# Four edits in the order of a decoder's big attention on one core: who splits the experts' weights, when a bias is added, who makes a chunk's low part, and where one sum P·V stands

## The chip, the cores and the metric

The kernel runs on one core of one Trainium2 chip. The metric is the device time of one execution in microseconds (us). Engines are named as in the profile: PE is TensorE's matmuls, PEld its weight loads, DVE VectorE, ACT ScalarE, POOL GpSimd (Pool), SP the engine that issues the DMAs.

## The reference

A decoder layer on x (16 sequences x 128 positions x 256), float32 throughout:

```python
x = _layernorm(x + attn(x, Wqkv, bqkv, Wo, bo))                   # A: 16 heads of 16
x = _layernorm(x + xattn(x, mask, ctx, Wq, Wk, Wv, Wo, gate))     # B: 32 heads of 8, gated adapter
x = _layernorm(x + ffn(x, ...))
# ffn: h = x + attention(layernorm(x)*w1 + b1)    16 heads of 128, rotary, causal softmax, biases
#      h + moe(layernorm(h)*w2 + b2)              4 experts 256 -> 256 -> 256, top 2, exact gelu
```

The change lies in the ffn's attention (the "big attention", stage C) and its passage to the experts (stage D).

## The kernel before

**Precision.** Where both sides of a product need float32 accuracy, each is kept as a high part (a copy rounded to fp32r by ScalarE) and a low part (value minus high part), and three products are summed: high x high, high x low, low x high. So the weights need a "split": `split_high` (L1709, ScalarE) and `split_low` (L1622, a subtraction of 128 x 1024 elements, by VectorE or Pool). The same is done for the normalized input of a chunk: `xt_pe` transposes it (L1454), `xt_act` scales it (L1472), `xh_act` makes the high part (L1479) and `xt_pool` the low part (L1486, two instructions of 128 x 512, t = 0 and 1).

**Stage C.** 64 units u = 0..63. A unit is one head (r = u % 16) on one chunk of four sequences (c = u // 16), 512 positions wide. The projections of head v run two units ahead, in unit v - 2. All engines walk the same loop over u, each through its own queue, in the order written, with semaphores between them:

- TensorE (`pe_c`): scores of u (L1526); transposition of the probabilities of u-1 (`turn`, L1540); query projection of u+2 (`project_c` with kq 0, L1497 to L1499, six products 128 x 512); output projection of u-2 (`out_proj`, L1566 to L1568); P·V of u-1 (`pv`, L1553); key projection of u+2 (kq 1); values of u+2 (L1513 to L1515). In a chunk's unit r = 14 the query projection belongs to the next chunk, whose input must first be there: it stands behind P·V. In r = 12 the next chunk's input is transposed.
- VectorE (`dve_c`): causal mask and row maxima of u (L1648, `maxima_c`); rotation with bias of the query projection (`rope_c` with kq 0, L1635 twice and L1638); after a chunk's end the residual (L1673); reciprocal of the sums (L1666); low part of the attention's output of u-1 (`out_low`, L1659); rotation of the key projection (kq 1); splits of the experts' weights in units 55 to 58; one step of the next chunk's layer norm for r = 4..11 (L1430 to L1443).
- ScalarE (`act_c`): copy of the transposed probabilities (L1718), exponentials (L1727), high part of the output (`out_high`, L1735), copy of the values (L1746), `split_high` in units 0 to 11 and 55 to 58, and for r = 12, 13 the next chunk's input and its high part.
- Pool (`pool_c`): the rotation's sum into the query buffer (`rope_sum_c`, L1794, kq 0), scaling of the probabilities (`soft`, L1802), the rotation's sum for the key; then `split_low` in units 0 to 11; `add_bias` (L1810, 128 x 256, one sequence); the power for the norm (L1449, r = 7); the low part of the next chunk's input (r = 13).

**What waits for what.** A projection or values product takes one of two PSUM banks in turn (`turn_bank`), and waits until the one before last in that order is read: the values of u+2 for the query's rotation, the query projection of u+3 for the key's rotation. `turn` waits for `soft`. P·V waits for ScalarE's copy, the high output for P·V, VectorE's low output for the high output. The first products of a chunk wait for both halves of the low part (`xt_ready`). The weights of the experts (DW) come in four halves (k = 16..19) through two staging buffers, the next load issued when a half is split. After the last chunk, unit 62 runs the first expert product (`hidden_pe`, L1930) in place of the values, which waits for the low part of chunk 4.

Of the kernel before, what the change touches and what calls it, by code (L numbers as in the profile page):

```python
# [6 lines left out]
F32 = mybir.dt.float32  # L7
F32R = mybir.dt.float32r
BF16 = mybir.dt.bfloat16
ALU = mybir.AluOpType  # L10
# [33 lines left out]
def program(nc, I, out):  # L44
    ctx = ExitStack()
    sem = Sems(nc, ctx)
# [998 lines left out]
    def pool_ab(e, steps):  # L1045
        q = Queue(e, sem)

        def init_values(b, n):

            if (b, n) in ((0, 0), (0, 1)):  # L1050
                q.wait_ge("w_dve", 4)
            elif (b, n) == (3, 1):
                q.wait_ge("z_dve", 16)
                q.wait_ge("rp_cos", 16)
            else:
                k = {(1, 0): 8, (1, 1): 6, (2, 0): 0, (2, 1): 2, (3, 0): 4}[b, n]
                for k in (k, k + 1):
                    q.wait_ge("pv_pe", last_unit(k + 10 if k < 6 else k, 0) + 1)
            k = 6 * (2 * b + n)
            vp = VPB[n][b].rearrange("p (t h) x -> p t h x", t=2)  # L1060
            e.memset(VPB[n][b], 0.0).then_inc(sem("z_B"), 1)
            q.wait_ge("z_B", k + 1)
            for i in range(3):
                e.memset(vp[:, :, i:12:3, 24 + i:25 + i], 1.0).then_inc(sem("z_B"), 1)
            e.memset(vp[:, 0, 12:16, 24:27:2], 1.0).then_inc(sem("z_B"), 1)
            e.memset(vp[:, 1, 12:16, 25:27], 1.0).then_inc(sem("z_B"), 1)

        def add_adapter(g):
            q.wait_ge("on_dve", on_v(out_group(g, 1), 4))
            e.tensor_tensor(ON[:, :], ON[:, :], OS, ALU.add).then_inc(sem("n_pool"), 1)  # L1070

        def mask_low(c):
            q.wait_ge("mkh_act", c - 7)
            if c >= 10:
                q.wait_ge("s_pe", last_unit(2 * (c - 2) + 1, 0) + 1)
            e.tensor_tensor(MKl[c % 2][:, :, :], MK[c % 2], MKh[c % 2][:, :, :].bitcast(F32), ALU.subtract).then_inc(sem("mkl_pool"), 1)

        def add_bias(g):
            q.wait_ge("ld_m", 48)
            q.wait_ge(f"ld_x{g // 2}", 16)  # L1080
            q.wait_ge("xt_pe", g // 2 + 1)
            e.tensor_tensor(X[:, g, :], X[:, g, :], boA, ALU.add).then_inc(sem("xb_pool"), 1)

        def weights_low(n):
            q.wait_ge("w_act", n + 1)
            e.tensor_tensor(Wl[0][:, :, piece(0, n)], staged(0, n), Wh[0][:, :, piece(0, n)].bitcast(F32),
                            ALU.subtract).then_inc(sem("w_pool"), 1)

        if steps.start < 0:
            for i in range(10):  # L1090
                e.memset(VPA[i], 0.0).then_inc(sem("z_A"), 1)
            q.wait_ge("z_A", 10)
            e.memset(VPOOL[:, 0:160, 16:17], 1.0).then_inc(sem("z_A"), 1)
        for s in steps:
            if s == 3 - AHEAD:
                weights_low(2)
            if s == 4 - AHEAD:
                weights_low(3)
            if s in INITS:
                init_values(*INITS[s])  # L1100
            if s - 1 in ends and ends[s - 1][0] < 16:
                add_bias(ends[s - 1][0])
            if s - 2 in tos and tos[s - 2][1]:
                add_adapter(tos[s - 2][0])
            if s - 2 in masked:
                mask_low(masked[s - 2][0])
            for part in range(2):
                if s in splits[part] and splits[part][s] not in FIRST:
                    split(e, q, *splits[part][s], part)
            if s in ropes and ropes[s][1] < 2 and ropes[s] not in FIRST:  # L1110
                rope(e, q, *ropes[s])
                if ropes[s][0] >= 9:
                    rope_cos(e, q, *ropes[s])
            if s in sums and sums[s][1] < 2 and sums[s] not in FIRST:
                rope_sum(e, q, *sums[s])
            if s in shifts and shifts[s] >= 16:
                shift_parts(e, q, shifts[s], "sh_pool")
            if s - 2 in wos:
                g = wos[s - 2]
                layernorm_power(e, q, g, "ln")  # L1120
                if g >= 16:
                    layernorm_apply(e, q, X[:, g - 16, :], z[:, :], g, "ln").then_inc(sem("x_done"), 1)
            if s == NORMS[3] + 1:
                norm_pool(e, q, 0)
            if s in NORMS[4:]:
                norm_step(e, q, 0, NORMS.index(s))
            if s in LOWS[:2]:
                split_low(e, q, LOWS.index(s))
            if s == X_LOW:
                for t in range(2):  # L1130
                    xt_pool(e, q, 0, t)
            for (v, kq), step in ROPES.items():
                if s == step:
                    rope_sum_c(e, q, v, kq)
# [161 lines left out]
    XF = [sb("C_XF", [128, 2, 512], F32, st_d)]  # L1296
    XCh = [sb("C_XTh", [128, 2, 512], F32R, st_d)]
# [60 lines left out]
    NU, NCH = 64, 4  # L1358
# [51 lines left out]
        return bank[4 + key[1]] if key[0] == "v" else home["cp", key[1], key[2]]  # L1410

    def xt_ready(c):
        return "xl_pool", 2 * c + 2

    def prep(u):

# [61 lines left out]
        q.wait_ge("xf_act", 2 * c + t + 1)  # L1478
        e.activation(XCh[i][:, t, :], XF[i][:, t, :], ACT.Copy).then_inc(sem("xh_act"), 1)  # L1479

    def xt_pool(e, q, c, t):
        i = 0 if c < 5 else c % 2
        if c == 0:
            q.wait_ge(*LEFT[1])
        q.wait_ge("xh_act", 2 * c + t + 1)
        e.tensor_tensor(XCl[i][:, t, :], XF[i][:, t, :], XCh[i][:, t, :].bitcast(F32), ALU.subtract).then_inc(sem("xl_pool"), 1)  # L1486

    def project_c(e, q, v, kq, o=None):
        c, r = divmod(v, 16)
# [39 lines left out]
    def pe_c(e):  # L1529
# [41 lines left out]
        for u in range(NU):  # L1571
            if u >= 2:
                scores_c(e, q, u)
            if u == NU - 1:
                gate_pe(e, q, 0)
            if u:
                turn(u - 1)
            if u == 0:
                q.wait_ge("z_dve", 32)
                q.wait_ge("rc_dve", 4)  # L1580
            if u + 2 < NU and u % 16 != 14:
                project_c(e, q, u + 2, 0)
            if u == NU - 1:
                hidden_pe(e, q, 0, 1)
            if u >= 2:
                out_proj(u - 2)
            if u:
                pv(u - 1)
            if u + 2 < NU and u % 16 == 14:
                project_c(e, q, u + 2, 0)  # L1590
            if u + 2 < NU:
                project_c(e, q, u + 2, 1)
                values_c(e, q, u + 2)
            else:
                hidden_pe(e, q, 0, 0 if u == NU - 2 else 2)
            if u % 16 == 12:

                q.wait_ge("oc_dve", u)
                for t in range(2):
                    xt_pe(e, q, u // 16 + 1, t, bank[2 + t])  # L1600
# [12 lines left out]
    def split_low(e, q, k):  # L1613
        hi, lo, src = half(k)
        if k in (2, 3):
            q.wait_ge(*LEFT[3])
        if k in (2, 4, 16):
            q.wait_ge("cw_low", k)
        if k in (16, 17):
            q.wait_ge("yc_pe", 54)  # L1620
        q.wait_ge("cw_act", k + 1)
        e.tensor_tensor(lo, src, hi.bitcast(F32), ALU.subtract).then_inc(sem("cw_low"), 1)  # L1622
# [29 lines left out]
    def dve_c(e):  # L1652
# [23 lines left out]
        for u in range(NU + 2):  # L1676
            c, r = divmod(u, 16)
            if 2 <= u < NU:
                maxima_c(e, q, u)
            if u == NU - 1:  # L1680
                gate_dve(e, q, 0, 0)
            if u + 2 < NU:
# [9 lines left out]
                    norm_step(e, q, 5, 4 * (u - NU + 2) + k)  # L1692
            if u + 2 < NU:
                rope_c(e, q, u + 2, 1)
            if c == 3 and 7 <= r <= 10:
                split_low(e, q, 16 + r - 7)
            if c < 4 and 4 <= r < 12:
                norm_step(e, q, c + 1, r - 4)
            if u == NU:
# [96 lines left out]
    def pool_c(e):  # L1796
# [15 lines left out]
        for u in range(NU):  # L1812
            c, r = divmod(u, 16)
            if u + 2 < NU:
                rope_sum_c(e, q, u + 2, 0)
            soft(u)
            if u + 2 < NU:
                rope_sum_c(e, q, u + 2, 1)
            if u < 12:
                split_low(e, q, 4 + u)  # L1820
            if 0 <= r - (8 if c else 12) < 4:
                add_bias(4 * c + r - (8 if c else 12))
            if r == 7:
                norm_pool(e, q, c + 1)
            if r == 13:
                for t in range(2):
                    xt_pool(e, q, c + 1, t)
            if u == NU - 2:
                norm_pool(e, q, 5)
        hidden_pool(e, q, 0, 0)  # L1830
        for m in range(1, 5):
            hidden_pool(e, q, 0, m)
        xt_pool(e, q, 5, 0)
        hidden_pool(e, q, 0, 5)
        xt_pool(e, q, 5, 1)
        hidden_pool(e, q, 0, 6)
        hidden_pool(e, q, 0, 7)

# [30 lines left out]
    XT_FIRST = 5  # L1869
# [288 lines left out]
    def pool_d(e):  # L2158
# [12 lines left out]
        for c in range(1, NCH):  # L2171
            for m in range(8):
                if c + 1 < NCH and XT_FIRST <= m < XT_FIRST + 2:
                    xt_pool(e, q, c + 5, m - XT_FIRST)
                hidden_pool(e, q, c, m)
                if c + 1 < NCH and m == 1:
                    norm_pool(e, q, c + 5)
# [187 lines left out]
```

## Time and profile before

| | us |
|---|---|
| three runs | 1230.07, 1232.98, 1234.13 |
| median | 1232.98 |
| the profiled execution | 1232.17 |
| its span (first to last instruction) | 1230.4 |
| mean granted TensorE clock | 0.985 |
| PE busy | 1146.7 (93%) |
| DVE busy | 986.4 (80%) |
| ACT busy | 656.9 (53%) |
| POOL busy | 660.3 (54%) |

Stage C runs from about 580 to 1100 us of the span. In the rows of the trace a line stands for all the buffers of a name; an entry in square brackets is the idle time of the engine before the instruction, and what ended it. An instruction's time on record can include a wait that the engine makes within it. "Unit u" begins in the text with its first scores product (L1526): unit 8 at 644.39, unit 13 at 684.68, unit 14 at 692.53, unit 15 at 704.66, unit 30 at 824.16, unit 31 at 834.79, unit 56 at 1036.44, unit 61 at 1083.40, unit 62 at 1091.25.

### The profile page before, as it was taken

The numbers are of one execution on the slowest core, as the hardware profiler recorded it, in microseconds if no ns is written. First come the engines' busy times: TensorE is split into PE (matmuls) and PEld (weight loads), VectorE is DVE, ScalarE is ACT, GpSimd is POOL, SyncE is SP. The second block draws the span as 40 slices with busy tenths as digits, with TensorE's granted clock in tenths as the row PEclk, the third lists the DMA queues.
The fourth block names the chain that finished last, engine by engine and source line by source line (L and its number), as shares of the span: only waits on it lengthen the run. The fifth ranks groups of instructions, "written<-read, shape, count | busy, mean of one in ns | idle before, by whom it ended". The sixth has DMA issues, their size and how long they took to land.

```text
span 1230.4 us, 29543 instructions
## 1 busy us (share of the span) xinstructions
PE 1146.7 (93%) x11172; PEld 938.6 (76%) x11172; DVE 986.4 (80%) x2274; ACT 656.9 (53%) x1687; POOL 660.3 (54%) x714
## 2 busy tenths in 40 slices
PE   5799999899999999878999999999999999899998
PEld 5676666566666666555899899988999898788886
DVE  6767786888888888967888688878888788966877
ACT  5365554566667667464555444453444444457663
POOL 4566556435455455253778544554455444556665
PEclk9899999999999999989999999999999999998999
DMA  8754543343333333302121000000000100001111
GB/s 228 184 133 116 125 122 84 84 103 103 94 103 102 95 101 88 106 18 78 61 69 53 1 1 2 1 2 1 1 2 1 35 2 18 19 3 35 35 35 35
DMA packets 98558, 76.22 MB, mean 62 GB/s; under 512 B 73547, under 2 KB 86987, under 8 KB 98417
## 3 DMA queue, kind: packets, MB, share of 16 engines
q1 hardware_dynamic: 98417, 74.34, 22.6%
q8 instruction: 89, 1.46, 0.5%
q14 instruction: 52, 0.43, 0.1%
HBM read 53.40 MB, written 19.92 MB: 60 GB/s over the span
## 4 chain that ended last, share of the span: by engine, by line
PE 61%; DVE 22%; issue 7%; ACT 4%; POOL 4%; DMA 1%; SPq 0%; DVEq 0%; POOLq 0%; ACTq 0%
PE bank L1497 4%; PE bank L1498 4%; PE bank L1499 4%; PE bank L607 4%; PE bank L1553 4%; PE bank L1526 4%; DVE B_nr L732 3%; DVE PT L741 3%; PE bank L543 3%; PE bank L550 2%; PE bank L470 2%; PE bank L1513 2%; PE bank L585 2%; PE bank L1515 2%; PE bank L1514 2%
## 5 line engine op out<-in xcount | busy, mean ns | idle before, releaser
L1794 POOL TENSOR_TENSOR C_QK<-C_t1b,C_t2b 128x512 f32<-128x512 f32 x128 | 167.0, 1305 | 240.6 <-DVE C_t2b L1638 240.4
L1635 DVE SCALAR_TENSOR_TENSOR C_t1b<-bank,C_bcol,C_tabs 64x512 f32<-64x512 f32 x256 | 192.0, 750 | 52.1 <-PE bank L1499 47.9
L732 DVE TENSOR_REDUCE B_nr<-bank 128x4 f32<-128x512 f32 x256 | 164.4, 684 | 34.4 <-PE bank L550 33.3
L1497 PE MATMUL bank<-C_XTh,C_Wh 128*128 128x512 f32 x256 | 113.7, 444 | 6.8 <-POOL C_XTl L1486 4.5
L972 ACT ACTIVATE PT<-bank 128x512 f32<-128x512 f32 x160 | 92.0, 597 | 50.7 <-PE bank L585 50.5
L1746 ACT ACTIVATE C_V<-bank 128x512 f32<-128x512 f32 x64 | 38.1, 598 | 149.2 <-PE bank L1515 147.6
L965 ACT ACTIVATE PT<-PT 128x512 f32<-128x512 f32 x96 | 59.5, 631 | 93.9 <-DVE PT L741 93.9
L1727 ACT ACTIVATE C_P<-bank,C_nm 128x128 f32<-128x128 f32 x256 | 90.7, 367 | 35.0 <-DVE C_nm L1648 33.3
L1498 PE MATMUL bank<-C_XTl,C_Wh 128*128 128x512 f32 x256 | 102.4, 400 | 0.0
L1499 PE MATMUL bank<-C_XTh,C_Wl 128*128 128x512 f32 x256 | 102.2, 399 | 0.0
L607 PE MATMUL bank<-PT,vpool 128*32 128x128 f32 x2048 | 97.3, 285 | 3.9 <-ACT PT L965 3.7
L1638 DVE SCALAR_TENSOR_TENSOR C_t2b<-bank,C_bcol,C_tabs 128x512 f32<-128x512 f32 x128 | 96.1, 751 | 1.8
L550 PEld LDWEIGHTS bank<-stk 48*128 48x128 bf16 (+1 forms) x1280 | 49.5, 95 | 47.3 <-issue 25.7
L585 PE MATMUL bank<-stk 54*128 54x128 bf16 (+1 forms) x1280 | 76.1, 218 | 7.2 <-DVE PT L741 5.0
L550 PE MATMUL bank<-stk 48*128 48x128 bf16 (+1 forms) x1280 | 76.2, 219 | 5.9 <-DVE B_nr L732 5.8
L1513 PE MATMUL bank<-C_Wh,C_XTh 128*128 128x256 f32 x256 | 72.9, 285 | 8.1 <-DVE C_t2b L1638 8.0
L1735 ACT ACTIVATE C_OTh<-bank,C_bcol 128x512 fp32r<-128x512 f32 x64 | 44.2, 690 | 66.6 <-PE bank L1553 65.8
L1659 DVE SCALAR_TENSOR_TENSOR C_OTl<-bank,C_bcol,C_OTh 128x512 fp32r<-128x512 f32 x64 | 47.7, 745 | 37.0 <-ACT C_OTh L1735 37.0
L438 POOL TENSOR_TENSOR PB<-y,PB 128x512 bf16<-128x512 f32 x37 | 43.3, 1170 | 56.0 <-ACT PB L916 55.7
L585 PEld LDWEIGHTS bank<-stk 54*128 54x128 bf16 (+1 forms) x1280 | 53.1, 95 | 25.4 <-DVE PT L741 8.2
L1514 PE MATMUL bank<-C_Wl,C_XTh 128*128 128x256 f32 x256 | 71.9, 281 | 0.0
L1566 PE MATMUL bank<-C_Wh,C_OTh 128*128 128x256 f32 x256 | 71.9, 281 | 0.0
(267 smaller groups left out, 3678.0 us busy)
## 6 DMA issues: line engine op xcount, KB each, us to landing
Adrq<-PB SPq DMA_DIRECT2D x16, 192.0 KB, 2.8
Adrk<-PB SPq DMA_DIRECT2D x16, 192.0 KB, 2.9
stk<-Adrq SPq DMA_DIRECT2D x16, 192.0 KB
stk<-Adrk SPq DMA_DIRECT2D x16, 192.0 KB
Bdrq<-PB SPq DMA_DIRECT2D x16, 192.0 KB, 2.9
stk<-Bdrq SPq DMA_DIRECT2D x32, 96.0 KB
Bdrk<-PB SPq DMA_DIRECT2D x16, 192.0 KB, 2.6
stk<-Bdrk SPq DMA_DIRECT2D x32, 96.0 KB
```

The source lines that it names most:

```text
L550: m = e.matmul(bank[n % 2][:, j * 128:j * 128 + 128], QS[L][i3][rows, h, :], (AS if kd else KS[L])[i3][rows, h, :], start=bool(kd), stop=b ...
L585: m = e.matmul(bank2(n)[:, j * 128:j * 128 + 128], (AS if kd else KS[L])[i3][rows, h, :], QS[L][i3][rows, h, :], start=bool(L), stop=bool( ...
L607: m = e.matmul(o[32 * j:32 * j + 32, c3 * 128:c3 * 128 + 128], vp[:, h, :], pt_of(n)[:, j * 128:j * 128 + 128], start=first or not L, stop ...
L732: e.tensor_reduce(dst, bank[n % 2][:, :].rearrange("p (a b) -> p a b", a=4), AX.X, ALU.max, negate=True).then_inc(sem("m_dve"), 1)
L1497: e.matmul(o[:, :], CWh[hp][:, cs], XCh[0][:, t, :], start=t == 0, stop=False)
L1498: e.matmul(o[:, :], CWh[hp][:, cs], XCl[0][:, t, :], start=False, stop=False)
L1499: m = e.matmul(o[:, :], CWl[hp][:, cs], XCh[0][:, t, :], start=False, stop=t == 1)
L1513: e.matmul(ob, XCh[0][:, t, xs], CWh[hp][:, cs], start=t == 0, stop=False)
L1514: e.matmul(ob, XCh[0][:, t, xs], CWl[hp][:, cs], start=False, stop=False)
L1635: e.scalar_tensor_tensor(out=v4(t1b[kq][lo:lo + 64, :]), in0=v4(o[hi:hi + 64, :]), scalar=bc[hi:hi + 64, :], in1=tabsC[hi:hi + 64, 2 * kq ...
L1638: e.scalar_tensor_tensor(out=v4(t2b[kq][:, :]), in0=v4(o[:, :]), scalar=bc, in1=tabsC[:, 2 * kq, :].unsqueeze(1).to_broadcast([128, 4, 128 ...
L1794: e.tensor_tensor(QK[v % 3][:, kq, :], t1b[kq][:, :], t2b[kq][:, :], ALU.add).then_inc(sem("rc_pool"), 1)
```

## The change

`xt_pool` becomes `xt_low` (semaphore `xl_done`) and can be issued by either engine. The rest, cut to its core:

```diff
 # pe_c
-            if u:
+            if u and (u % 16 != 14 or u + 2 >= NU):
                 pv(u - 1)
             if u + 2 < NU and u % 16 == 14:
                 project_c(e, q, u + 2, 0)
             if u + 2 < NU:
                 project_c(e, q, u + 2, 1)
+                if u % 16 == 14:
+                    pv(u - 1)
                 values_c(e, q, u + 2)
 # split_low
-        if k in (2, 4, 16):
+        if k in (2, 4):
             q.wait_ge("cw_low", k)
 # dve_c
                 maxima_c(e, q, u)
+            if r == 14:
+                xt_low(e, q, c + 1, 1)
             ...
                 rope_c(e, q, u + 2, 1)
-            if c == 3 and 7 <= r <= 10:
-                split_low(e, q, 16 + r - 7)
 # pool_c
                 split_low(e, q, 4 + u)
-            if 0 <= r - (8 if c else 12) < 4:
-                add_bias(4 * c + r - (8 if c else 12))
+            if c == 3 and 7 <= r <= 10:
+                split_low(e, q, 16 + r - 7)
             if r == 7:
                 norm_pool(e, q, c + 1)
             if r == 13:
-                for t in range(2):
-                    xt_pool(e, q, c + 1, t)
+                xt_low(e, q, c + 1, 0)
+            if 0 <= r - (0 if c else 12) < 4:
+                add_bias(4 * c + r - (0 if c else 12))
```

So: the four low parts of the experts' weights are made by Pool; the output bias is added to the residual rows in r = 0..3 of chunks 1 to 3 (in chunk 0 still in r = 12..15, but behind the low part); of the next chunk's low part Pool makes t = 0 in r = 13 and VectorE t = 1 in r = 14, behind its maxima; and in r = 14 of chunks 0 to 2 P·V stands behind both projections, in front of the values.

## Rows read from the trace of the kernel before

**Rows 1.** The page, part 4: the chain that ended last, by engine.
```profile
PE 61%; DVE 22%; issue 7%; ACT 4%; POOL 4%; DMA 1%; SPq 0%; DVEq 0%; POOLq 0%; ACTq 0%
```
**Rows 2.** Stretches (length, busy us (instructions) of each engine, PEclk, DMA).
```profile
644.39:684.68 40.29, 40.29 (x290) 37.48 (x289) 35.19 (x89) 21.83 (x62) 31.13 (x21) 1.00 0.15 42
1036.44:1083.40 46.96, 42.34 (x290) 37.25 (x289) 43.54 (x93) 20.55 (x61) 24.80 (x20) 1.00 0.08 24
684.68:692.53 7.85, 7.85 (x59) 7.30 (x57) 5.59 (x16) 4.07 (x12) 4.27 (x4) 1.00 0.00 0
692.53:704.66 12.13, 9.93 (x59) 8.44 (x57) 5.96 (x17) 4.22 (x13) 5.92 (x6) 0.86 0.01 1
...
824.16:834.79 10.63, 8.40 (x59) 7.31 (x58) 5.97 (x17) 4.22 (x13) 5.25 (x5) 1.00 0.01 2
...
954.29:964.91 10.62, 8.39 (x58) 7.31 (x57) 5.97 (x17) 4.22 (x13) 5.25 (x5) 1.00 0.33 101
```
**Rows 3.** Waits of PE in stage C: total, times, longest.
```profile
PE bank L1513 <- DVE C_t2b L1638: 8.0, 8, 1.2
```
**Rows 4.** Line L1622, the low part of weights: ns min/median/max, first and last start.
```profile
L1622 POOL TENSOR_TENSOR C_Wl<-C_z,C_Wh x6: 2375/2390/2397, 592.1 to 670.7; 128x1024 fp32r<-128x1024 f32 x6
```
**Rows 5.** Timeline of Pool and VectorE, unit 56 (start, duration, instruction).
```profile
1047.23 1.29 POOL L1794 TENSOR_TENSOR C_QK<-C_t1b,C_t2b 128x512 f32<-128x512 f32 x1 [0.74 <-DVE C_t2b L1638]
1048.48 1.73 POOL L1810 TENSOR_TENSOR X<-X,C_bo 128x256 f32<-128x256 f32 x1
...
1047.47 2.13 DVE L1622 TENSOR_TENSOR C_Wl<-C_XF,C_Wh 128x1024 fp32r<-128x1024 f32 x1 [0.32 <-ACT C_Wh L1709]
```
**Rows 6.** VectorE's subtractions of two widths, before stage C, by line and form.
```profile
L714 DVE TENSOR_TENSOR B_Wl<-vpool,B_Wh 128x1024 fp32r<-128x1024 f32 x2 | 2.4, 1220 | 1.9 <-ACT B_Wh L862 1.9
...
L714 DVE TENSOR_TENSOR A_Wl<-stk,A_Wh 128x512 fp32r<-128x512 f32 x2 | 1.3, 682 | 0.0
```
**Rows 7.** Timelines of unit 30: TensorE, VectorE, ScalarE, Pool.
```profile
826.91 1.05 PE L1553 MATMUL bank<-C_PT,C_V 128*128 128x128 f32 x8
829.22 0.50 PE L1497 MATMUL bank<-C_XTh,C_Wh 128*128 128x512 f32 x1 [1.26 <-POOL C_XTl L1486]
...
833.27 0.39 PE L1513 MATMUL bank<-C_Wh,C_XTh 128*128 128x256 f32 x1 [0.97 <-DVE C_t2b L1638]
...
826.22 0.14 DVE L1648 DVE_READ_ACCUMULATOR2_ANT C_nm<- 128x1 f32 x1
...
833.21 0.72 DVE L1659 SCALAR_TENSOR_TENSOR C_OTl<-bank,C_bcol,C_OTh 128x512 fp32r<-128x512 f32 x1
833.97 0.76 DVE L1635 SCALAR_TENSOR_TENSOR C_t1b<-bank,C_bcol,C_tabs 64x512 f32<-64x512 f32 x1
...
828.00 0.69 ACT L1735 ACTIVATE C_OTh<-bank,C_bcol 128x512 fp32r<-128x512 f32 x1
...
825.42 1.30 POOL L1794 TENSOR_TENSOR C_QK<-C_t1b,C_t2b 128x512 f32<-128x512 f32 x1 [1.50 <-DVE C_t2b L1638]
826.67 2.50 POOL L1486 TENSOR_TENSOR C_XTl<-C_XF,C_XTh 128x512 fp32r<-128x512 f32 x2
```
**Rows 8.** The same of unit 14: Pool, VectorE, TensorE.
```profile
693.78 1.30 POOL L1794 TENSOR_TENSOR C_QK<-C_t1b,C_t2b 128x512 f32<-128x512 f32 x1 [1.50 <-DVE C_t2b L1638]
695.04 0.72 POOL L1810 TENSOR_TENSOR X<-X,C_bo 128x256 f32<-128x256 f32 x1
...
703.84 0.76 DVE L1635 SCALAR_TENSOR_TENSOR C_t1b<-bank,C_bcol,C_tabs 64x512 f32<-64x512 f32 x1
...
698.26 0.50 PE L1497 MATMUL bank<-C_XTh,C_Wh 128*128 128x512 f32 x1 [1.93 <-POOL C_XTl L1486]
...
703.14 0.39 PE L1513 MATMUL bank<-C_Wh,C_XTh 128*128 128x256 f32 x1 [0.27 <-DVE C_t2b L1638]
```
**Rows 9.** The same of unit 62: Pool, TensorE.
```profile
1092.50 1.29 POOL L1794 TENSOR_TENSOR C_QK<-C_t1b,C_t2b 128x512 f32<-128x512 f32 x1 [1.50 <-DVE C_t2b L1638]
...
1096.30 0.50 PE L1930 MATMUL bank<-C_XTh,C_Wh 128*128 128x512 f32 x1 [1.26 <-POOL C_XTl L1486]
```

More of the change, by code:

```diff
@@ L1130, in pool_ab @@
                 for t in range(2):
-                    xt_pool(e, q, 0, t)
+                    xt_low(e, q, 0, t)
             for (v, kq), step in ROPES.items():
@@ L1412, in xt_ready @@
     def xt_ready(c):
-        return "xl_pool", 2 * c + 2
+        return "xl_done", 2 * c + 2
     def prep(u):
@@ L1479, in xh_act, with xt_low @@
         e.activation(XCh[i][:, t, :], XF[i][:, t, :], ACT.Copy).then_inc(sem("xh_act"), 1)
-    def xt_pool(e, q, c, t):
+    def xt_low(e, q, c, t):
         i = 0 if c < 5 else c % 2
@@ L1485, in xt_pool @@
         q.wait_ge("xh_act", 2 * c + t + 1)
-        e.tensor_tensor(XCl[i][:, t, :], XF[i][:, t, :], XCh[i][:, t, :].bitcast(F32), ALU.subtract).then_inc(sem("xl_pool"), 1)
+        e.tensor_tensor(XCl[i][:, t, :], XF[i][:, t, :], XCh[i][:, t, :].bitcast(F32), ALU.subtract).then_inc(sem("xl_done"), 1)
     def project_c(e, q, v, kq, o=None):
@@ L1832, in pool_c @@
             hidden_pool(e, q, 0, m)
-        xt_pool(e, q, 5, 0)
+        xt_low(e, q, 5, 0)
         hidden_pool(e, q, 0, 5)
-        xt_pool(e, q, 5, 1)
+        xt_low(e, q, 5, 1)
         hidden_pool(e, q, 0, 6)
@@ L2173, in pool_d @@
                 if c + 1 < NCH and XT_FIRST <= m < XT_FIRST + 2:
-                    xt_pool(e, q, c + 5, m - XT_FIRST)
+                    xt_low(e, q, c + 5, m - XT_FIRST)
                 hidden_pool(e, q, c, m)
```

## The prediction

> **What bounds the kernel now.** I read the page's busy shares and chain first, then the stretches of the big attention, then TensorE's waits there, then single units. The chain of work that ended last is 61% TensorE and 22% VectorE [rows 1]. A regular unit of the big attention takes 7.85 us, with 7.85 us of TensorE in it [rows 2]: so there only what makes TensorE stand still counts. It stands still in two places that the change touches. It waits 8.0 us in all at the value products (L1513) for VectorE's rotation [rows 3], and 1.93 us [rows 8] and 1.26 us [rows 7] at the first projection of a chunk (L1497) for Pool's low part. The stretches [rows 2] say when. Units 56 to 60 take 46.96 us, while units 8 to 12, with the same 290 products, take 40.29. And the last-but-one unit of a chunk takes 12.13, 10.63 and 10.62 us instead of 7.85.
>
> **The experts' weights (four splits from VectorE to Pool in units 55 to 58).** The same rows price it, because before the change the units 7 to 11 already have the new arrangement: Pool runs one split of 2.39 us in each [rows 4], right behind the second rotation sum, ScalarE makes the high part in front of it, and VectorE does the normalization steps of the next chunk beside. Stretch against stretch: 46.96 - 40.29 = 6.67 us saved [rows 2]. TensorE's value product no longer waits, because VectorE's order (maxima, rotation, low output, rotation) is no longer shifted by the split (2.13 us for the second one [rows 5]). What hides Pool's 2.39 us is Pool's own idle time: 31.13 us busy of 40.29 with the splits in place. The heaviest moment is the first split, with the power of the norm now queued behind it; its twin is inside the stretch too, since what Pool does last in unit 7 runs after the scores of unit 8 have begun. The twin stretch has five splits, the new one will have four. No wait is new in front of the split: it stands behind a rotation sum that needs a later projection than the out product it waits for. The load of the next half of the weights is issued after the split as in the first chunk. Bounds of this term: 7.7 (46.96 less five regular units of 7.85) and -8.1 (four splits of 2.39 and the rotation sums of 1.30 behind them, all exposed).
>
> **Bias in a chunk's first units.** Four additions of 0.72 us on Pool move from r = 8..11 to r = 0..3 in chunks 1 to 3. Pool idles 1.5 us or more before its rotation sums in both places, and what reads the biased rows (the residual) comes in the next chunk. 0, between -0.1 and +0.3. In chunk 0 the addition of r = 13 goes behind the low part, which is in the next step.
>
> **Low part in halves, one on VectorE.** Chunk 1 to 2 first [rows 7]. Pool's rotation sum ends at 826.72, then come both halves, 2.50 us, and the first projection starts at 829.22. VectorE has finished its maxima at 826.36 and is then idle until that projection, so the half costs VectorE nothing. If the halves ran side by side, the low part would be done at 826.72 + 1.25 = 827.97. But both instructions read two operands from SBUF, and the trace shows what happens then [rows 5]: VectorE's split starts at 1047.47 under a Pool addition that ends at 1048.52, and ends at 1049.60, 1.08 us after it, though it is on record as 2.13 us; Pool's bias, queued at 1048.48, ends at 1050.21, 0.61 us after VectorE let go, though it takes 0.72 alone. They exclude each other. So: VectorE's half is queued at 826.38 behind the running Pool sum. It runs after 826.72 for 1.08 us less the difference between 1024 and 512 columns (1.22 - 0.68 = 0.54 [rows 6]), to 827.26. Pool's half follows, 1.25 - 0.11 = 1.14 us, to 828.40; the projection starts 0.05 later, at 828.45: 0.77 us earlier, not 1.20.
>
> The Trainium skill (SBUF — State Buffer, section Who interferes with whom) has this as an exclusive lock between a VectorE instruction with two SBUF inputs and a GpSimd one that reads SBUF, given to whoever issues first. The trace agrees on the exclusion by the 1.08 us. If Pool's half got it first, the end would be 827.97 + 0.54 = 828.51, 0.11 later; without any exclusion it would be 827.97.
>
> **The sum P·V placed later.** In unit 30 TensorE now does both projections (3.08 us, 829.22 to 832.30 before, so 828.45 to 831.53), then P·V (1.05 us, overlapping 0.16: to 832.42). Behind P·V hang ScalarE's high output (starts 0.04 later, 0.69 us: 833.15) and VectorE's low output (0.72 us, from 833.18 to 833.90), and in VectorE's queue the second rotation stands behind that low output: it starts at 833.94. Before it started at 833.97. TensorE's next projection needs the bank that this rotation reads. So of the 0.77 us nothing is left: 0.03 us a boundary, for chunks 1 to 2 and 2 to 3. TensorE's 0.97 us wait before the value products goes, and a wait of about 1 us in front of the next unit's projection takes its place. With P·V in its old place the second rotation would keep its distance of 4.75 us from the first projection (829.22 to 833.97) and start at 833.20.
>
> Chunk 0 to 1 [rows 8]: Pool's sum ends at 695.08, and the bias (0.72 us) is out of the way. VectorE's half to 695.62, Pool's to 696.76, projection at 696.81 instead of 698.26. The idle time of TensorE becomes 1.4 us instead of 1.93, and I take it that the clock stays up: the granted share was 0.86 in this unit and 1.00 in unit 30, where it had idled 1.26 and 0.97 [rows 2, 7]. Then: projections to 699.89, P·V to 700.78, high output to 701.51, low output to 702.26, second rotation at 702.30 instead of 703.84: 1.54 us saved.
>
> End of chunk 3 [rows 9]: P·V stays in its place there. Pool's sum ends at 1093.79, VectorE's half at 1094.33, Pool's at 1095.47, first hidden product at 1095.52 instead of 1096.30: 0.78 us. What follows (last scores, gate, transposition, exponentials) is a chain through TensorE and ScalarE, so it is kept.
>
> **The sum.** 6.67 + 1.54 + 2 x 0.03 + 0.78 = 9.05 us. The profiled execution took 1232.17 us (span 1230.40), so it becomes 1223.1. The median of the three runs shown is 0.8 above it (1232.98); I go half way: 1223.5.
>
> **Rivals.** (a) The halves do run side by side: 0.43 us more at each of four places, 9.05 + 1.7 = 10.8 us, 1221.8. For it: VectorE is free at the right moment; against it: rows 5. (b) The clock falls at the boundaries. TensorE idles 1.4 us before the projection (out product's end 827.07 to 828.45) and about 1 us again five us later. Twelve projection products took 4.61 us in chunk 0 (698.26 to 702.87) and 3.08 at full clock, so 1.5 us for each of three boundaries: 1225.0 for one, 1228.1 for all. Against it: 1.26 followed by 0.97 us did not bring it down [rows 2, 7]. (c) Pool is too full in units 55 to 58: its soft-max scaling, which releases the transposition, stands behind the split. Its work there is 31.13 / 5 = 6.2 us of a unit's 8.1; a split that waits over some 1.9 us for its high part, or for the lock, pushes the scaling out and stops TensorE. Exposed in part, 1.5 us a unit, it gives 1229.5, which can't be told from no change. (d) The slower case, the same place at full price: Pool's split (2.39) and the rotation sum queued behind it (1.30) are both exposed in all four units, 3.69 x 4 = 14.8 us; 14.8 - 9.05 = +5.7, 1238.3. It outweighs the rest once a unit grows by over 9.05 / 4 = 2.3 us, so once Pool's wait passes 1.9 + 2.3 = 4.2 us. Against (c) and (d): units 8 to 12 of the first chunk [rows 2].
>
> **Numbers.** Forecast 0.58, (a) 0.13, (b) 0.18, (c) 0.06, (d) 0.02, and 0.03 for something between forecast and no change. The range: 1220.3 (side by side, less the spread of the runs) to 1228.1 (the clock at all boundaries). 0.3%, about what a measurement of this kernel tells from no change, is 3.7 us. Faster by more: 0.92 (forecast, a, b and the rest), same 0.06, slower 0.02.
>
> **What would show it.** After the change units 56 to 60 should take 40.3 us, and TensorE's wait at L1513 for the rotation should be near zero. VectorE's half should be on record with about 0.9 us (0.34 of it a wait) and Pool's with some 1.7. In unit 30 the value products should begin about 0.8 us earlier, and so the long unit be 9.9 us instead of 10.63, but the first projection of unit 31 not: that unit should be as much longer. Units 14 and 15 together should lose 1.5 us. I am wrong on the lock if both halves show their plain 0.68 and 1.25 us, on P·V if the second rotation after a boundary is 0.5 us earlier or more, on the clock if the granted share in the long units of chunks 1 and 2 is under 1.00, and on Pool if TensorE waits at the transposition (L1540) for the scaling.

## The result

| | before | changed |
|---|---|---|
| four runs each, median (range) | 1232.20 (1230.07 to 1234.13) | 1220.74 (1218.70 to 1223.33) |
| ratio, 95% interval | | 0.9909 [0.9883, 0.9934] |
| profiled execution | 1232.17 | 1221.01 |
| its span | 1230.4 | 1219.2 |
| timed again, 11 and 6 runs | 1231.40 | 1224.29 |
| ratio, 95% interval | | 0.9940 [0.9926, 0.9953] |

The change is faster by 11.5 us in one comparison and 7.1 us in the other, 0.9% and 0.6% of the time; 9.05 was the sum and 1223.5 the forecast. The profiles say where the time went. These are stretches of the changed kernel, cut at the first scores product of a unit as in [rows 2] (length, busy us (instructions) of PE, PEld, DVE, ACT and POOL, PEclk, DMA share, GB/s): the first chunk's units 8 to 12, units 56 to 60, then 14, 15, 30, 31, unit 62, all that is before stage C, and all that follows the last scores.

```profile
643.43:683.73 40.30, 40.30 (x290) 37.48 (x289) 35.21 (x89) 21.79 (x62) 31.12 (x21) 1.00 0.14 41
1033.94:1074.05 40.11, 40.11 (x291) 37.38 (x289) 35.20 (x89) 20.97 (x61) 28.76 (x20) 1.00 0.10 28
...
691.58:701.41 9.83, 8.38 (x58) 7.45 (x57) 6.24 (x17) 4.22 (x13) 5.16 (x5) 1.00 0.01 2
701.41:710.30 8.89, 8.12 (x59) 7.35 (x58) 7.38 (x18) 3.39 (x11) 5.08 (x5) 1.00 0.00 1
821.70:831.53 9.83, 8.38 (x59) 7.44 (x58) 6.24 (x17) 4.22 (x13) 4.47 (x4) 1.00 0.01 3
831.53:840.41 8.88, 8.11 (x58) 7.34 (x57) 7.37 (x18) 3.39 (x11) 4.37 (x4) 1.00 0.00 1
...
1081.89:1087.66 5.77, 5.29 (x40) 4.85 (x39) 4.44 (x15) 4.22 (x13) 3.97 (x3) 1.00 0.00 0
0.00:579.02 579.02, 520.57 (x6896) 372.20 (x6897) 459.80 (x937) 344.64 (x839) 298.06 (x402) 0.98 0.41 108
1087.66:1219.20 131.54, 123.32 (x763) 105.10 (x761) 99.22 (x261) 77.90 (x123) 79.05 (x82) 0.97 0.10 33
```

The same view of the kernel before, where it was not shown: before stage C, units 15 and 31, and the end.

```profile
0.00:579.96 579.96, 520.45 (x6897) 372.39 (x6898) 460.77 (x937) 344.06 (x839) 297.02 (x402) 0.98 0.41 108
704.66:712.80 8.14, 8.14 (x59) 7.35 (x58) 6.64 (x17) 3.39 (x11) 5.08 (x5) 1.00 0.00 1
834.79:842.92 8.13, 8.11 (x59) 7.34 (x58) 6.63 (x17) 3.40 (x11) 4.37 (x4) 1.00 0.00 1
...
1097.80:1230.38 132.58, 124.67 (x763) 106.25 (x761) 97.25 (x258) 77.96 (x123) 79.11 (x82) 0.96 0.10 33
```

| stretch | before | changed | difference | forecast |
|---|---|---|---|---|
| units 56 to 60 | 46.96 | 40.11 | -6.85 | -6.67 |
| 14 + 15 (chunk 0 to 1) | 20.27 | 18.72 | -1.55 | -1.54 |
| 30 + 31 (chunk 1 to 2) | 18.76 | 18.71 | -0.05 | -0.03 |
| 46 + 47 (chunk 2 to 3) | 18.74 | 18.73 | -0.01 | -0.03 |
| unit 62 | 6.55 | 5.77 | -0.78 | -0.78 |
| before stage C | 579.96 | 579.02 | -0.94 | 0 |
| after the last scores | 132.58 | 131.54 | -1.04 | 0 |

Stage C gave 9.24 us. Only part of the 6.85 us of units 56 to 60 is idle time of TensorE: it stood still for 4.62 us in this stretch before ([rows 2], length less PE busy); the other 2.23 us are in the recorded time of the same products, 42.34 us before and 40.11 after. A sum of waits would have missed them, the comparison of stretches did not.

The other 2 us of this profile lie where the change does nothing. The work there is the same, but for three short instructions of VectorE that were done before the last scores and now come behind them; TensorE's instructions keep their distance from the last scores to 0.01 us for the next 14 us, so the 0.78 us of unit 62 is kept. What differs in the last stretch is the granted clock, 0.96 against 0.97, with PE busy 124.67 against 123.32 us. In the ten other profiles the part before stage C took 577.6 to 581.3 us and the part after the last scores 130.8 to 133.0. That is no effect of the change: the changed kernel itself, in the profile of the second comparison, took 581.16 and 132.85 us there, and its stage C is the same to 0.1 us in every stretch of the table. So 9.2 us is what the change does in stage C, and 7 to 11 is what single comparisons of whole runs show of it. The interval of the second comparison (5.8 to 9.1 us) ends just short of 9.2; why whole runs gave less there than in the first comparison isn't settled beyond these two stretches.

Unit 30 of the changed kernel, to set beside [rows 7] (start, duration, instruction; in brackets the idle time before it). All of it lies 2.47 us earlier, by what was saved up to there.

```profile
825.97 0.50 PE L1497 MATMUL bank<-C_XTh,C_Wh 128*128 128x512 f32 x1 [1.37 <-POOL C_XTl L1486]
...
828.87 1.05 PE L1553 MATMUL bank<-C_PT,C_V 128*128 128x128 f32 x8
830.01 0.39 PE L1513 MATMUL bank<-C_Wh,C_XTh 128*128 128x256 f32 x1
...
833.79 0.50 PE L1497 MATMUL bank<-C_XTh,C_Wh 128*128 128x512 f32 x1 [0.77 <-DVE C_t2b L1640]
```
```profile
823.75 1.04 DVE L1486 TENSOR_TENSOR C_XTl<-C_XF,C_XTh 128x512 fp32r<-128x512 f32 x1
...
830.68 0.75 DVE L1661 SCALAR_TENSOR_TENSOR C_OTl<-bank,C_bcol,C_OTh 128x512 fp32r<-128x512 f32 x1 [0.64 <-ACT C_OTh L1737]
831.46 1.51 DVE L1637 SCALAR_TENSOR_TENSOR C_t1b<-bank,C_bcol,C_tabs 64x512 f32<-64x512 f32 x2
```
```profile
829.96 0.69 ACT L1737 ACTIVATE C_OTh<-bank,C_bcol 128x512 fp32r<-128x512 f32 x1 [4.53 <-PE bank L1553]
```
```profile
822.95 1.30 POOL L1796 TENSOR_TENSOR C_QK<-C_t1b,C_t2b 128x512 f32<-128x512 f32 x1 [1.50 <-DVE C_t2b L1640]
824.20 1.72 POOL L1486 TENSOR_TENSOR C_XTl<-C_XF,C_XTh 128x512 fp32r<-128x512 f32 x1
```

The reader is to see three things. VectorE's half is on record from 823.75 to 824.79, but Pool's rotation sum ran until 824.25: 0.54 us behind it, as worked out. (It had been queued before VectorE's last maxima instruction was through, so it is on record with 1.04 us, not the 0.9 that was forecast.) Pool's half takes 1.72 us instead of 1.25 and ends at 825.92; the first projection starts at 825.97, which is 828.44 in the time of before (forecast 828.45). VectorE's second rotation starts at 831.46, 833.93 in the time of before (forecast 833.94). The wait before the values (0.97) has become one before the next unit's projection (0.77). TensorE's waits in stage C, of which L1513 was 8.0 us [rows 3]:

```profile
PE bank L1497 <- POOL C_XTl L1486: 4.1, 3, 1.4
PE bank L1497 <- DVE C_t2b L1640: 3.1, 6, 0.8
PE bank L1513 <- DVE C_t2b L1640: 1.3, 1, 1.3
```

The wait that is left at L1513 lies at 587.57 us, at the start of stage C, where the kernel before had one of 1.23 us too; the seven others are gone.

### The profile page after: what moved, and what is told of

It is laid out like the page before. It is cut to its first block, busy times and chain, and to the rows that moved or that the text cites. A ratio compares the mean times of both kernels' runs of the same rounds, so it can differ in the third digit from the quotient of the medians.

```text
span 1219.2 us, 29543 instructions
## 1 busy us (share of the span) xinstructions
PE 1141.6 (94%) x11172; PEld 936.7 (77%) x11172; DVE 982.3 (81%) x2274; ACT 657.6 (54%) x1687; POOL 664.7 (55%) x714
## 4 chain that ended last, share of the span: by engine, by line
PE 63%; DVE 21%; issue 7%; ACT 4%; POOL 4%; DMA 1%; SPq 1%; DVEq 0%; POOLq 0%; ACTq 0%
PE bank L1497 5%; PE bank L1498 5%; PE bank L1499 5%; PE bank L1553 4%; PE bank L1526 4%; PE bank L607 4%; DVE B_nr L732 3%; DVE PT L741 3%; PE bank L543 3%; PE bank L550 2%; PE bank L470 2%; PE bank L1568 2%; PE bank L1567 2%; PE bank L1566 2%; PE bank L585 2%
## 5 line engine op out<-in xcount | busy, mean ns | idle before, releaser
L1637 DVE SCALAR_TENSOR_TENSOR C_t1b<-bank,C_bcol,C_tabs 64x512 f32<-64x512 f32 x256 | 192.0, 750 | 45.5 <-PE bank L1499 41.5
L1513 PE MATMUL bank<-C_Wh,C_XTh 128*128 128x256 f32 x256 | 72.5, 283 | 1.6 <-DVE C_t2b L1640 1.3
```

Of the source, the lines that this page charges most:

```text
L1637: e.scalar_tensor_tensor(out=v4(t1b[kq][lo:lo + 64, :]), in0=v4(o[hi:hi + 64, :]), scalar=bc[hi:hi + 64, :], in1=tabsC[hi:hi + 64, 2 * kq ...
```

## The experiments

Each is the changed kernel with the edit shown. The compared quantity is the length of the stretches, since it doesn't move with the clock of the other stages. Where no median is given, the version ran once.

**P·V back in front of the projections.**
```diff
-            if u and (u % 16 != 14 or u + 2 >= NU):
+            if u:
                 pv(u - 1)
 ...
-                if u % 16 == 14:
-                    pv(u - 1)
                 values_c(e, q, u + 2)
```


> The changed kernel with P·V of r = 14 back in front of the projections. My theory (the second rotation hangs on P·V through the high and the low output): the first projection of a chunk starts where it does in the changed kernel, but the second rotation starts 4.75 us after it instead of 5.5, so units 14+15, 30+31 and 46+47 are 0.75 us shorter each (18.0 instead of 18.7 us), 2.2 us in all: about 1218.5. Rival (the late P·V fills TensorE's wait before the values and so is worth it): the same or up to 1 us a boundary longer.

Units 14+15, 30+31 and 46+47 (18.72 us in the changed kernel, forecast 18.0):

```profile
693.92:711.88 17.96, 16.51 (x114) 14.65 (x113) 13.50 (x34) 7.62 (x24) 10.25 (x9) 1.00 0.00 1
823.24:841.21 17.97, 16.52 (x115) 14.66 (x114) 13.51 (x34) 7.62 (x24) 8.85 (x7) 1.00 0.01 2
952.61:970.58 17.97, 16.52 (x114) 14.65 (x113) 13.49 (x34) 7.62 (x24) 8.86 (x7) 1.00 0.19 59
```

The place of P·V costs 0.75 us at each boundary. The median of 4 runs is 1219.94 (forecast 1218.5), ratio to before 0.9905 [0.9889, 0.9922]; the whole times alone don't part it from the changed kernel (0.9909), the stretches do. Unit 30 itself, from 823.24 to 833.09, is as long as with P·V late (9.85 against 9.83 us); it is unit 31 that is shorter, 8.12 against 8.88. TensorE waits longer in front of the values now, 0.97 us at each of the three boundaries (the fourth wait, 1.24 us, is the one at the start of stage C), and is faster all the same, because it waits less at the projections:

```profile
PE bank L1513 <- DVE C_t2b L1638: 4.2, 4, 1.2
PE bank L1497 <- POOL C_XTl L1486: 1.4, 3, 0.5
PE bank L1497 <- DVE C_t2b L1638: 0.8, 3, 0.3
```

**The four splits back on VectorE.**
```diff
 # pool_c
-            if c == 3 and 7 <= r <= 10:
-                split_low(e, q, 16 + r - 7)
 # dve_c, behind the key's rotation
+            if c == 3 and 7 <= r <= 10:
+                split_low(e, q, 16 + r - 7)
 ...
```
(`split_low` waits for `cw_low` at k = 16 again, as before.)

> The changed kernel with the experts' four low parts back on VectorE. My theory: units 56 to 60 take 47.0 us again instead of 40.1, +6.8 us, nothing else moves. Rival (part of the gain there came from the bias being gone from the same units, r = 8 to 11, where it was held up by VectorE's splits): 45.5 us or less.

Units 56 to 60:

```profile
1034.88:1080.55 45.67, 42.35 (x290) 37.25 (x289) 42.27 (x93) 20.54 (x61) 19.04 (x16) 1.00 0.08 24
```

That is neither the 47.0 of my theory nor quite the rival's 45.5. The rival is right in kind: 1.29 us of the 6.85 are gained without moving a split, by the bias alone. The normalization step shows how. Before, and in this run (VectorE, unit 56, one execution each):

```profile
1049.53 0.83 DVE L1443 TENSOR_SCALAR C_XN<-X,mv,rstd 128x256 f32<-128x256 f32 x1
```
```profile
1047.96 0.40 DVE L1443 TENSOR_SCALAR C_XN<-X,mv,rstd 128x256 f32<-128x256 f32 x1
```

Before, Pool's bias waited behind the split [rows 5] and was over at 1050.21, 0.61 us after the split; the step is on record from 1049.53 to 1050.36, and I read its extra 0.43 us as a wait for the bias in turn. The same pair stands in units 56, 57 and 58; in unit 59, where the bias has no split in front of it, the step takes 0.41 us. Three times 0.43 us are 1.29.

**Bias back in r = 8 to 11, splits on Pool.**
```diff
-            if 0 <= r - (0 if c else 12) < 4:
-                add_bias(4 * c + r - (0 if c else 12))
+            if 0 <= r - (8 if c else 12) < 4:
+                add_bias(4 * c + r - (8 if c else 12))
```


> The changed kernel with the bias of chunks 1 to 3 back in r = 8 to 11 (the splits stay on Pool). The run with the splits on VectorE took 45.7 us for units 56 to 60 and not 47.0, with VectorE's normalization step at 0.40 us instead of 0.83: the bias had held the exclusive access that VectorE's split had let go. My theory: with the splits on Pool the step is issued in front of Pool's rotation sum, the bias comes 4 us later and falls into idle time, so units 56 to 60 take 40.1 to 40.3 us and the bias's new place is worth nothing here. Rival (Pool is now so full that 0.72 us more delays its scaling): TensorE waits at the transposition (L1540), 41 us or more.

Units 56 to 60: 40.13 us. Pool is busy 31.39 us in them instead of 28.76, and TensorE without a pause:

```profile
1033.61:1073.74 40.13, 40.13 (x290) 37.40 (x289) 35.19 (x89) 20.96 (x61) 31.39 (x24) 1.00 0.09 28
```

So with the splits on Pool the bias's place is worth nothing in these units, and the splits alone bring the whole 6.8 us. The two edits don't add up: either one removes what the bias did. Nor does the new place cost anything: units 16 to 19, 32 to 35 and 48 to 51 of the changed kernel are as long as before, to 0.02 us each.

**Both halves of the low part on Pool.**
```diff
 # pool_c, r == 13
-                xt_low(e, q, c + 1, 0)
+                for t in range(2):
+                    xt_low(e, q, c + 1, t)
 # dve_c
-            if r == 14:
-                xt_low(e, q, c + 1, 1)
```


> The changed kernel with both halves of the low part on Pool in r = 13 (P·V late). My theory: Pool needs 2.50 us where the two engines need 1.72, so each first projection starts 0.78 us later, and with P·V late all of it is kept: units 30+31 take 19.5 us, which is 0.75 more than even before the change; four places, +3.1 us. If TensorE's idle time of 2.2 us lets its clock fall, 1.5 us more at a boundary. Rival (the second rotation is held by something else than P·V): units 30+31 stay at 18.7.

Units 14+15, 30+31 and 46+47:

```profile
692.50:713.55 21.05, 17.78 (x115) 15.87 (x114) 12.71 (x33) 7.62 (x24) 11.00 (x10) 0.92 0.00 1
824.95:846.01 21.06, 17.80 (x115) 15.98 (x114) 12.71 (x33) 7.62 (x24) 9.61 (x8) 0.92 0.01 2
957.38:976.88 19.50, 16.51 (x114) 14.80 (x113) 12.72 (x33) 7.62 (x24) 9.62 (x8) 1.00 0.17 55
```

The third is the forecast of 19.5 to the digit: 0.77 us over the changed kernel and 0.76 over the kernel before. So the late P·V by itself, with nothing else changed there, makes a boundary slower than it was. In the other two the granted clock fell to 0.92 over the two units, 1.55 us more. All three had the same pause of TensorE in front of the projection, 2.15, 2.14 and 2.14 us:

```profile
962.43 0.50 PE L1497 MATMUL bank<-C_XTh,C_Wh 128*128 128x512 f32 x1 [2.14 <-POOL C_XTl L1486]
```

That is rival (b) of the prediction, in one execution. With the low part in halves the pause is 1.37 us (P·V late) or shorter, and the granted share was 1.00 at every boundary of all eight profiles with halves. The halves are the only edit between this version and the changed kernel, so they are what spared it the longer pause; putting P·V back would have done so too (1.26 us in unit 30 of the kernel before, share 1.00). At the end of chunk 3 unit 62 took 6.55 us here, as before the change, so its 0.78 us are the halves' alone.

**Pool's half in front of the rotation sum, P·V in its old place.**
```diff
 # pool_c (and the P·V edit of the first experiment)
             soft(u)
+            if r == 13:
+                xt_low(e, q, c + 1, 0)
             if u + 2 < NU:
                 rope_sum_c(e, q, u + 2, 1)
-            if r == 13:
-                xt_low(e, q, c + 1, 0)
```


> The changed kernel with P·V in its old place and, in r = 13, Pool's half of the low part in front of the rotation sum of the key instead of behind it (the sum is needed a unit later only). My theory (what delays the low part is the rotation sum in front of it and the exclusion between Pool and VectorE behind it): Pool's half runs while VectorE still makes the maxima, VectorE's half follows, the low part is done before P·V is, and TensorE doesn't wait for it: units 30+31 take 17.3 us instead of 18.7, three times 1.4, and 0.6 at the end of chunk 3: 4.8 us under the changed kernel, about 1216. Rival (the rotation sum, now later, holds up the next scores or the scaling): TensorE waits at the scores (L1526) or the transposition (L1540), and less or nothing is gained.

Units 30+31 (forecast 17.3); 14+15 and 46+47 took 17.23 and 17.22, units 61+62 12.88 (13.62 in the changed kernel):

```profile
818.80:836.02 17.22, 16.24 (x114) 14.58 (x113) 13.64 (x34) 7.62 (x24) 8.87 (x7) 1.00 0.01 2
```

TensorE's wait for the low part is gone; neither the scores nor the transposition waits, but for 0.6 us at the start of stage C that the kernel before has too. Pool and VectorE in unit 30:

```profile
820.19 1.30 POOL L1486 TENSOR_TENSOR C_XTl<-C_XF,C_XTh 128x512 fp32r<-128x512 f32 x1 [1.64 <-ACT C_XTh L1479]
821.45 1.73 POOL L1794 TENSOR_TENSOR C_QK<-C_t1b,C_t2b 128x512 f32<-128x512 f32 x1
```
```profile
820.85 1.19 DVE L1486 TENSOR_TENSOR C_XTl<-C_XF,C_XTh 128x512 fp32r<-128x512 f32 x1
```

VectorE's half ends 0.55 us after Pool's (821.49 to 822.04), once more by the exclusion, and now it is the rotation sum that is held up, for which nobody waits yet. Median 1217.14 (forecast 1216), ratio to before 0.9886 [0.9871, 0.9901]. What the place in front would bring with both halves on Pool was not run.

**The same with P·V late.** (The edit of `pool_c` alone.)

> Pool's half of the low part in front of the key's rotation sum, as in the run before, but with P·V late as in the changed kernel. My theory: the first projection starts 0.26 us sooner than with P·V in front, but the second rotation hangs on P·V (projections, P·V, high output, low output) and starts 0.5 us later: units 30+31 take 17.75 us against 17.22; units 61+62 12.87 as there. Rival (with the low part early the order of P·V makes no difference, or the late one is better since TensorE's 0.98 us wait before the values is filled): 17.2 or less.

Units 30+31, and to 0.01 us the same at the other two boundaries, as forecast; units 61+62 12.87:

```profile
819.47:837.23 17.76, 16.52 (x114) 14.78 (x113) 13.75 (x34) 7.61 (x24) 8.87 (x7) 1.00 0.01 2
```

So the late P·V costs here too, 0.53 us. (Its single run was 1215.28 us, lower than the medians of the version above: its last stretch had the clock at 0.98 and took 130.8 us, where the version above took 133.0.)

**Both halves on VectorE, P·V in its old place.**
```diff
 # dve_c, r == 14
-                xt_low(e, q, c + 1, 1)
+                for t in range(2):
+                    xt_low(e, q, c + 1, t)
 # pool_c: nothing in r == 13
```


> Both halves of the low part on VectorE in r = 14, P·V in its old place. My theory (VectorE waits until Pool's rotation sum is through, then needs 0.54 + 0.68 us, where VectorE and Pool need 0.54 + 1.14): the first projection starts 0.45 us earlier than with one half each, units 30+31 take 17.5 us against 17.96, units 61+62 13.2 against 13.6. Rival (no exclusion, VectorE starts at once): 17.3 or less. Rival (VectorE's extra work delays the maxima or rotation): 18 or more.

Units 30+31 and 46+47: 17.45 us (forecast 17.5), 61+62 13.09 (13.2). Units 14+15 took 17.97, a miss of 0.5: only there Pool has its bias queued behind the rotation sum (r = 13 of chunk 0). VectorE's two halves are on record as one line, and so is the bias:

```profile
693.77 2.18 DVE L1486 TENSOR_TENSOR C_XTl<-C_XF,C_XTh 128x512 fp32r<-128x512 f32 x2
694.22 1.18 POOL L1811 TENSOR_TENSOR X<-X,C_bo 128x256 f32<-128x256 f32 x1
```

The rotation sum ends at 694.27, the bias at 695.40, VectorE's second half at 695.95, 0.55 us after the bias. That fits an order of first half (to about 694.81), bias, second half: here the waiting Pool instruction came in between two of VectorE's that stood in a row. It is the one place where it was seen.

**The two versions timed together.**

> The changed kernel itself, timed beside the next one on the same chip: 1220.5 to 1222.5, 10 to 11 us under the kernel before (my working: 9.05 us, with 9.2 found in stage C and its passage; the rest is where the clock falls in stage D).

> Pool's half in front of the rotation sum and P·V in its old place, timed in more rounds. By the unit sums (3 x 1.49 and 0.75 us under the changed kernel) it is 5.2 us faster than the changed kernel; the medians of the shorter runs were 3.6 apart. My theory: 4 to 6 us under the changed kernel in the same call. Rival (what is saved in stage C is given back in stage D, where the clock falls at another place): 2 us or less.

Medians 1224.29 (6 runs) and 1216.49 (4 runs), ratios to the kernel before 0.9940 [0.9926, 0.9953] and 0.9880 [0.9867, 0.9893]. Both expectations missed, the changed kernel by 1.8 us to the slow side and the difference of the two, 7.8 us where 4 to 6 was expected, by 1.8 as well. The stretches are the same as in the first profiles (18.72 and 17.22 us a boundary). By them the second version is 5.2 us faster (3 x 1.50 and 0.75). In the two profiled executions the rest lies in the part before stage C and in the last stretch, where the clock differs: 581.16 and 579.68, 132.85 and 131.36 us, 3.0 us between them. That these stretches also explain the medians (7.8 apart here, 3.6 before, from two different comparisons) is likely but not shown, since only one execution of each was profiled. The second version beats both kernels, with an interval that doesn't touch theirs.

## Why the prediction was right

- **The splits, 6.67 us.** Measured 6.85, all of it by the splits (bias experiment). The twin units of the first chunk were the right price, since they carried the same neighbours. The forecast was 0.18 us low: units 8 and 10 of the twin took 7.91 and 7.90 us where units 56 and 58 now take 7.84 each. The twin has one split more; whether that is why isn't shown.
- **The bias, 0.** Right for the change as it stands. But the reading beneath it was too simple: I took Pool's idle time and the reader of the rows as the only questions, and in the kernel before the bias cost 1.3 us, by my reading through the exclusion of VectorE's normalization step. Moved without the splits it would have been worth 1.29 us, not 0. [Rows 5] showed that bias at 1.73 us; I used the row for the low part and didn't ask who stood behind it.
- **The halves.** The exclusion was read from two rows, and the forecasts of 0.54 us for VectorE and 1.14 for Pool held to 0.02. VectorE's half was queued a little earlier than I had it (1.04 us on record for 0.9), which changed nothing. Rival (a), side by side, is refuted by every profile with halves.
- **P·V late.** That it eats the gain of the halves at chunks 1 to 2 and 2 to 3 was forecast to within 0.02 us, and the first experiment shows it is P·V and not something else. The wait that was filled (0.97 us before the values) was not the one that decided; VectorE's queue was. At chunk 0 to 1 the late P·V costs as much, 0.76 us (18.72 against 17.96), and is hidden in the forecast's 1.54. About 0.8 us of that gain are the clock's, an estimate: there the second rotation came 5.58 us after the first projection before the change (698.26 to 703.84), at full clock in unit 30 it came 4.75 after.
- **The clock, rival (b).** Not met, rightly left out, and real: with a pause of 2.15 us instead of 1.37 the clock fell at two boundaries of three, and its price, forecast at 1.5 us, was 1.55. In unit 14 the pause went from 1.93 to 1.36 us and the granted clock from 0.86 to 1.00.
- **Pool too full, (c) and (d).** Not met: TensorE is busy without a pause in units 56 to 60 even with 31.4 us of Pool's work.
- **What the sum lacked.** 2 us of the first comparison came from stretches outside the change. I gave the range 1.5 us for that spread at the lower end, and the last stretch and the first alone differ by 2.2 and 3.7 us from profile to profile. So it is partly luck how near the time came: the first median, 1220.74, is 0.4 us from the lower end and nearer to rival (a)'s 1221.8 than to the forecast, the second, 1224.29, is on the forecast's other side. What bears the forecast out are the stretches, not the median.

## What to carry to other kernels

Before work is moved into an engine's pause to fill it, follow what hangs on the moved work through the other queues: here P·V filled a pause of 1 us, the unit came out no shorter, and the next one grew by 0.76 us. Halving a job between VectorE and Pool gave less than half where both read two operands from SBUF: the low part was done 1.67 us after Pool's rotation sum instead of 2.45. To let Pool's half jump a neighbour that nobody waited for yet brought nearly as much again: with P·V in its old place units 30 and 31 went from 18.76 to 17.97 us by the halves, and to 17.22 by the jump. And where a kernel has a stretch with the same neighbours as the one you change, its length is a better price than any sum of instruction times.

## What the runs showed of the hardware

In one execution the same pause of TensorE, 2.14 to 2.15 us in the same surroundings, was followed by a fall of the granted clock at two boundaries and not at the third, for 1.55 us each; pauses of 1.36 or 1.37 us, at twelve boundaries in four profiles, never were. And an instruction's recorded time held a wait for the other engine in both directions: VectorE's 128 x 512 subtraction was on record with 1.04 and 1.19 us where it takes 0.68, Pool's with 1.72 where it takes 1.25. What the blocked instruction still needed once the other was through was 0.54 to 0.55 us for VectorE's 512 columns and 1.13 to 1.14 for Pool's.
